# Attention and low-rank FFN block on one core: keys' transposes moved behind the product of probabilities and values, and two PSUM banks exchanged

## The reference

```
x  = x + attn(layernorm(x))          # one pre-norm block
x  = x + ffn(layernorm(x))

attn: xn = layernorm(x) * ln_g + ln_b
      q, k, v = split(xn @ W_qkv + b_qkv);  gate = sigmoid(x @ W_gate + b_gate)
      gate = gate / (mean(gate) + EPS)
      q = relu(q * gate)**2 + EPS;  k = relu(k * gate)**2 + EPS   # 16 heads of 32
      causal linear attention: state += k v^T, sums += k
      out = (q . state) / (q . sums + EPS);  out @ W_proj + b_proj
ffn:  P = x @ U1;  H = gelu(P @ V1 + b1);  Q = H @ U2;  Q @ V2 + b2   # rank 128, 2048 wide
```

## Time and profile before

| what | before |
|---|---|
| median of 3 runs | 1751.72 us (1750.33 to 1752.75) |
| the profiled execution | 1750.89 us |
| its span | 1749.2 us |
| granted TensorE clock, mean | 0.997 |
| matmul / weight load | busy 98% / 82% of the span |
| VectorE / ScalarE / GpSimd | busy 77% / 38% / 52% |
| chain that ended last | TensorE 83%, VectorE 6%, GpSimd 6%, issue 3%, ScalarE 2% |
| an even step with all its parts | 25.37 us (29 of them, all within 25.19 to 25.39) |
| an odd step with all its parts | 27.77 us (29 of them, 27.74 to 27.79) |

### The profile page before, as it was taken

How to read it: one execution, slowest core, us unless ns; L and a number is a source line. 1 busy time by engine, 2 the same in 40 slices (tenths; PEclk the granted TensorE clock), 3 DMA queues, 4 the chain that set the end, 5 groups by cost and what they waited for, 6 DMA issues and landing times.

```text
span 1749.2 us, 39518 instructions
## 1 busy us (share of the span) xinstructions
PE 1714.2 (98%) x16477; PEld 1429.6 (82%) x16477; DVE 1345.2 (77%) x2159; ACT 665.5 (38%) x1242; POOL 911.4 (52%) x1026
## 2 busy tenths in 40 slices
PE   6899999999999999999999999999999999999997
PEld 4788888888888888888888888888888888888886
DVE  7887777877877777777778777778777777777775
ACT  4243343343333343433433433333333434334332
POOL 3355555555555555555555555555555555555540
PEclk9999999999999999999999999999999999999999
DMA  7111111011111111110111111111111111101100
GB/s 218 58 35 52 34 53 45 28 53 53 33 53 39 35 52 36 49 52 23 51 52 33 53 40 33 52 52 34 52 35 39 53 36 50 52 22 52 40 19 25
DMA packets 61937, 82.09 MB, mean 47 GB/s; under 512 B 14952, under 2 KB 25600, under 8 KB 61760
## 3 DMA queue, kind: packets, MB, share of 16 engines
q1 hardware_dynamic: 60896, 77.99, 14.0%
q10 hardware_dynamic: 864, 1.57, 0.3%
HBM read 62.60 MB, written 16.94 MB: 45 GB/s over the span
## 4 chain that ended last, share of the span: by engine, by line
PE 83%; DVE 6%; POOL 6%; issue 3%; ACT 2%; DMA 0%; SPq 0%; DVEq 0%; POOLq 0%
PE ps_a L822 8%; PE ps_a L823 8%; PE ps_a L824 8%; PE scores L822 8%; PE scores L823 8%; PE scores L824 8%; POOL h_lo L432 6%; PE scores L829 5%; PE ps_h L822 5%; PE scores L956 4%; PE scores L991 4%; PE ps_h L823 3%; PE ps_h L824 3%; PE ps_q L822 3%; PE ps_q L824 2%
## 5 line engine op out<-in xcount | busy, mean ns | idle before, releaser
L432 POOL TENSOR_TENSOR h_lo<-h_full,h_hi 128x512 fp32r<-128x512 f32 x244 | 352.0, 1457 | 234.7 <-DVE h_hi L654 234.7
L515 ACT ACTIVATE h_full<-ps_h,cols 128x256 f32<-128x256 f32 x512 | 207.3, 477 | 20.3 <-PE ps_h L824 19.6
L822 PE MATMUL scores<-wx_hi,zt_hi 128*128 128x512 f32 x512 | 207.2, 405 | 6.9 <-DVE key_sums L762 4.3
L822 PE MATMUL ps_a<-wx_hi,zt_hi 128*128 128x512 f32 x512 | 208.4, 407 | 0.0
L823 PE MATMUL scores<-wx_lo,zt_hi 128*128 128x512 f32 x512 | 203.6, 398 | 0.0
L824 PE MATMUL scores<-wx_hi,zt_lo 128*128 128x512 f32 x512 | 203.4, 397 | 0.0
L823 PE MATMUL ps_a<-wx_lo,zt_hi 128*128 128x512 f32 x512 | 202.1, 395 | 0.0
L824 PE MATMUL ps_a<-wx_hi,zt_lo 128*128 128x512 f32 x512 | 201.9, 394 | 0.0
L452 POOL TENSOR_TENSOR key_lo<-keys,key_hi 128x512 fp32r<-128x512 f32 x64 | 83.2, 1300 | 191.1 <-ACT key_hi L550 191.1
L654 DVE CAST h_hi<-h_full 128x512 fp32r<-128x512 f32 x256 | 165.0, 672 | 10.3 <-ACT h_full L515 10.3
L526 ACT ACTIVATE query_t<-scores 128x512 f32<-128x512 f32 x64 | 38.3, 598 | 346.6 <-PE scores L829 346.6
(11 more groups left out here) (158 smaller groups left out, 4283.0 us busy)
## 6 DMA issues: line engine op xcount, KB each, us to landing
xs<-L_attn_x SPq DMA_DIRECT2D x64, 256.0 KB, 4.1
out<-x1s SPq DMA_DIRECT2D x64, 256.0 KB, 2.1
xt<-x_turned SPq DMA_DIRECT2D x63, 256.0 KB, 4.2
key_sums<-carry_rows SPq DMA_DIRECT2D x60, 256.0 KB, 3.8
rows<-turned_rows SPq DMA_DIRECT2D x63, 64.0 KB, 4.8
x1s<-L_attn_W_gate SPq DMA_DIRECT2D x4, 256.0 KB, 3.9
x1s<-L_ffn_U SPq DMA_DIRECT2D x4, 256.0 KB, 7.0
carry_rows<-key_sums SPq DMA_DIRECT2D x64, 2.0 KB
```

Source lines behind the costliest of these rows:

```text
L432: E.tensor_tensor(h_lo[:, i % SLOTS, :], h_full[:, i % SLOTS, :], h_hi[:, i % SLOTS, :].bitcast(F32), ALU.subtract).then_inc(s["h_lo_ready ...
L515: last = E.activation(h_full[:, i % SLOTS, a * GROUP:(a + 1) * GROUP], ps_h[i % 2][:, a * GROUP:(a + 1) * GROUP], ACT.Gelu_apprx_tanh, bia ...
L822: E.matmul(ps, wh, mh, start=start and i == 0, stop=False)
```

## The change

Four things are moved. The keys' transposes and ScalarE's copy `key_t` are done one step ahead, for chunk `n` instead of `c`: TensorE transposes directly behind the product of probabilities and values, into `ps_a`, waiting for `value_ready` and `key_ready`; ScalarE copies behind `ot_hi`. Banks `ps_a` and `ps_b` are exchanged for GATE, KEY, QUERY, the causal sums and the output projection (VALUE stays in `ps_a`). The scores therefore wait for the keys' evacuation instead of the queries', and the VALUE projection for the queries'; the sums wait for `key_t_ready` instead of `ot_ready`. In even steps a second h pair comes ahead of the scores instead of behind them. On VectorE the first cast to `h_hi` (in even steps the first two) comes directly behind `probs`, ahead of the values.

```diff
@@ scalar, step @@
-                if c.exists:
-                    act.wait_ge(s["tk_done"], c.done())
-                    E.activation(key_t[:, :, :].rearrange(flat), ps_t[:, :], ACT.Copy)\
-                        .then_inc(s["key_t_ready"], 1)
...
                     E.activation(ot_hi[:, :, :], out_cols, ACT.Copy)\
                         .then_inc(s["ot_hi_ready"], 1)
+                if n.exists:
+                    act.wait_ge(s["tk_done"], n.done())
+                    E.activation(key_t[:, :, :].rearrange(flat), ps_a[:, :], ACT.Copy)\
+                        .then_inc(s["key_t_ready"], 1)
                 z_head(Chunk(p, b + 1))
@@ vector, step @@
                         .then_inc(s["probs_ready"], 1)
+                if ffn.exists:
+                    h_head(ffn, pairs[0], finishing)
+                    if b % 2 == 0:
+                        h_head(ffn, pairs[1], finishing)
...
-                if ffn.exists:
-                    h_head(ffn, pairs[0], finishing)
                 if c.exists:
                     dve.wait_ge(s["ot_hi_ready"], c.done())
...
                 z_tail(Chunk(p, b + 1))
                 if ffn.exists:
-                    h_head(ffn, pairs[1], finishing)
+                    if b % 2:
+                        h_head(ffn, pairs[1], finishing)
@@ tensor, step @@
-                    project(GATE, ps_b, s["gate_done"])
+                    project(GATE, ps_a, s["gate_done"])
...
-                    project(KEY, ps_a, s["key_done"])
+                    project(KEY, ps_b, s["key_done"])
...
-                    project(QUERY, ps_b, s["query_done"])
-                if c.exists:
-
-                    if d.exists:
-                        pe.wait_ge(s["x1t_ready"], d.done())
-                    else:
-                        pe.wait_ge(s["query_t_ready"], c.done())
-                    pe.wait_ge(s["key_ready"], c.done())
-                    transpose4(keys[:, c.half, :], s["tk_done"])
+                    project(QUERY, ps_a, s["query_done"])
...
                 if ffn.exists and b % 2 == 0:
                     h_pair(ffn, pairs[0])
+                    h_pair(ffn, pairs[1])
                 if c.exists:
 
                     if n.exists:
-                        pe.wait_ge(s["query_steps"], n.done(3, 1))
-                    else:
-                        pe.wait_ge(s["den_steps"], c.done(6, 1))
+                        pe.wait_ge(s["key_steps"], n.done(3, 1))
+                    elif d.exists:
+                        pe.wait_ge(s["x1_steps"], d.done(3, 1))
                     pe.wait_ge(s["key_t_ready"], c.done())
+                    pe.wait_ge(s["query_t_ready"], c.done())
+                    if d.exists:
+                        pe.wait_ge(s["x1t_ready"], d.done())
...
-                if ffn.exists:
-                    h_pair(ffn, pairs[0 if b % 2 else 1])
+                if ffn.exists and b % 2:
+                    h_pair(ffn, pairs[0])
...
-                    pe.wait_ge(s["key_steps"], n.done(3, 1))
+                    pe.wait_ge(s["query_steps"], n.done(3, 1))
                     project(VALUE, ps_a, s["value_done"])
...
                     mm.then_inc(s["ot_done"], 1)
+                if n.exists:
+                    pe.wait_ge(s["value_ready"], n.done())
+                    pe.wait_ge(s["key_ready"], n.done())
+                    transpose4(keys[:, n.half, :], s["tk_done"], ps_a)
...
-                    if c.exists:
-                        pe.wait_ge(s["ot_ready"], c.done())
-                    else:
-                        pe.wait_ge(s["query_steps"], n.done(3, 1))
+                    pe.wait_ge(s["key_t_ready"], n.done())
                     pe.wait_ge(s["key_lo_ready"], n.done())
-                    E.matmul(ps_b[:, :], causal_r[:, :], key_hi[:, :], start=True, stop=False)
+                    E.matmul(ps_a[:, :], causal_r[:, :], key_hi[:, :], start=True, stop=False)
...
-                    product(ps_a[:, :], [(ot_hi[:, k, :], ot_lo[:, k, :]) for k in range(KT)],
+                    product(ps_b[:, :], [(ot_hi[:, k, :], ot_lo[:, k, :]) for k in range(KT)],
```

More of the change, by code:

```diff
@@ L679, in step @@
                     dve.wait_ge(s["x_small"], n.done(5, 2))
-                    E.scalar_tensor_tensor(out=gate[:, :], in0=ps_b[:, :], scalar=small[:, n.slot, 1:2],
+                    E.scalar_tensor_tensor(out=gate[:, :], in0=ps_a[:, :], scalar=small[:, n.slot, 1:2],
                                            in1=bias[:, GATE, :], op0=ALU.mult, op1=ALU.add)\
@@ L692, in step @@
                         add_rows(0)
-                    squared_relu(n, s["key_done"], s["key_steps"], ps_a, KEY, keys[:, n.half, :],
+                    squared_relu(n, s["key_done"], s["key_steps"], ps_b, KEY, keys[:, n.half, :],
                                  x1t_tail)
@@ L711, in step @@
                         add_rows(1)
-                    squared_relu(n, s["query_done"], s["query_steps"], ps_b, QUERY, queries[:, :])
+                    squared_relu(n, s["query_done"], s["query_steps"], ps_a, QUERY, queries[:, :])
                 if b % 2 and ffn.exists:
@@ L789, in step @@
                         dve.wait_ge(stored[c.slot], before.dmas())
-                    E.tensor_tensor(x1s[:, c.slot, :], ps_a[:, :], xs[:, c.slot, :], ALU.add)\
+                    E.tensor_tensor(x1s[:, c.slot, :], ps_b[:, :], xs[:, c.slot, :], ALU.add)\
                         .then_inc(s["x1_steps"], 1)
@@ L825, in product, with transpose4 @@
                 return mm
-            def transpose4(src, done):
+            def transpose4(src, done, ps=ps_t):
                 for k in range(KT):
-                    mm = E.transpose(ps_t[:, k * P:(k + 1) * P], src[:, k * P:(k + 1) * P], ident[:, :])
+                    mm = E.transpose(ps[:, k * P:(k + 1) * P], src[:, k * P:(k + 1) * P], ident[:, :])
                 mm.then_inc(done, 1)
@@ L996, in step @@
                     mm.then_inc(s["ot_done"], 1)
+                if n.exists:
+                    pe.wait_ge(s["value_ready"], n.done())
+                    pe.wait_ge(s["key_ready"], n.done())
+                    transpose4(keys[:, n.half, :], s["tk_done"], ps_a)
                 if ffn.exists:
-                    if b % 2:
-                        h_pair(ffn, pairs[1])
-                    h_pair(ffn, pairs[2])
-                    if b % 2 == 0:
-                        h_pair(ffn, pairs[3])
+                    h_pair(ffn, pairs[1 if b % 2 else 2])
+                    h_pair(ffn, pairs[2 if b % 2 else 3])
                 if n.exists:
-                    if c.exists:
-                        pe.wait_ge(s["ot_ready"], c.done())
-                    else:
-                        pe.wait_ge(s["query_steps"], n.done(3, 1))
+                    pe.wait_ge(s["key_t_ready"], n.done())
                     pe.wait_ge(s["key_lo_ready"], n.done())
-                    E.matmul(ps_b[:, :], causal_r[:, :], key_hi[:, :], start=True, stop=False)
-                    E.matmul(ps_b[:, :], causal_r[:, :], key_lo[:, :], start=False, stop=True)\
+                    E.matmul(ps_a[:, :], causal_r[:, :], key_hi[:, :], start=True, stop=False)
+                    E.matmul(ps_a[:, :], causal_r[:, :], key_lo[:, :], start=False, stop=True)\
                         .then_inc(s["sums_done"], 1)
```

8 lines of the change are left out of this document (2 added, 6 removed).

## The result

| what | before | after |
|---|---|---|
| median of the runs | 1751.24 us (6, 1750.33 to 1752.75) | 1744.18 us (6, 1743.48 to 1744.5) |
| ratio after / before | | 0.9958, 95% interval 0.9945 to 0.997 |
| the profiled execution, its span | 1750.89, 1749.2 | 1743.48, 1741.7 |
| an even step | 25.37 | 24.76 |
| an odd step | 27.77 | 28.19 |

The kernel is 7.1 us (0.4%) faster by the medians and 7.5 us by the two spans. It is less than the even steps alone gained: 30 x 0.61 = 18.3 us, of which 31 odd steps of +0.42 took 13 back; the ends gave the other 2. All lengths of steps and parts here are means over the 29 even and 29 odd steps with all their parts, as distances between two starts; within one kernel they scatter by a few hundredths, but for single even steps of the kernel before and of e11, up to 0.2 us shorter than the others.

A forecast was written before the change was run, and what follows sets the result against it. TensorE, busy 1714.2 of 1749.2 us, was taken as the bound; 30 even steps by -0.60, 31 odd by +0.51 and -3 for the ends sum to -5.2 us, from 1751.7 to 1747 us, range 1738 to 1757.

The forecast's parts named there:

- even: transposes and their wait taken out ahead of the scores: Even step, ahead of the scores: the four transposes gone, -0.44 us, and the wait for `key_t` gone, -0.13 us.
- even: transposes behind the product: Even step, behind the product of probabilities and values: the four transposes put in cost +0.44 us, bounds +0.34 and +0.64.
- even: sums without `ot_lo`: Even step, the sums' first matmul: it no longer waits for `ot_lo`, -0.11 us.
- even: u2 products: Even step, u2 products: early casts let GpSimd's last `h_lo` end some 1.5 us earlier, removing a wait, -0.36 us.
- odd: gain left ahead of the first h pair: Odd step, scores to first h pair: `pt_lo` on VectorE leaves only 0.10 of the transposes' 0.44 us as gain.
- odd: gelu behind `ot_hi`: Odd step, last h pair: its gelu comes later by 0.49 us for copy `key_t` and about 0.12 for the transposes.
- ends: First and last steps: about -2 us in step 64, -1 in steps 1 and 2; together -3.
- Rival (d): Around the moved transposes: the change of products costs twice, +0.2 us in both kinds of step; 1759 us, chance 0.06.
- the +0.12 for `key_t` waiting on the transposes: Odd step, ScalarE: `key_t` cannot start before the transposes are done, making the last h pair's gelu about 0.12 us later.
- (a): Even step, VectorE: early casts meet GpSimd, values come late and TensorE's transposes wait; 1756 us with one held, chance 0.12.
- (b): Odd step: the last h pair's new wait does not come, the gelu being done in time; 1731 us, chance 0.10.
- (c): Even step: last `h_lo` stays late, held by GpSimd or delayed gelus, so 0.36 us stays; 1758 us, chance 0.07.

The follow-up runs named there:

- e11: The kernel before with only banks `ps_a` and `ps_b` exchanged and the waits that follow; 1750.35 us, ratio 0.9991 to before.
- e1: The kernel after with the keys' transposes and copy `key_t` back at their old place behind the QUERY projection; 1736.43 us, ratio 0.991 to before.
- e3: The kernel after with `pt_lo` put ahead of the queries' third operation on VectorE in odd steps; 1734.33 us, ratio 0.9897 to before.
- e2: The kernel after with the second pair's gelu put ahead of `zt_hi` on ScalarE in odd steps; 1752.97 us, ratio 1.0006 to before.
- e6: The kernel before with only the early casts to `h_hi` moved directly behind the masking; 1741.45 us, ratio 0.994 to before.
- e9: The kernel after; in odd steps second pair's gelu ahead of `zt_hi`, its cast ahead of `zt_lo`, `pt_lo` ahead of the queries' third operation; 1734.45 us.
- e12: The kernel after; odd steps: second pair's gelu ahead of `zt_hi`, second and third pairs' casts ahead of `zt_lo`, `pt_lo` before queries' third operation; 1728.07 us.

## Why the prediction was right, point by point

The forecast was a change of -5.2 us against the profiled execution; the spans differ by -7.5, and the median, 1744.18, lies 2.8 below the 1747 said and inside the range. The even step came as worked out, the odd one by the waits that were worked out and a little cheaper.

| term | forecast | measured |
|---|---|---|
| even: transposes and their wait taken out ahead of the scores | -0.57 | -0.57 |
| even: transposes behind the product | +0.44 | +0.41 |
| even: sums without `ot_lo` | -0.11 | -0.11 |
| even: u2 products | -0.36 | -0.34 |
| **even step** | **-0.60** | **-0.61** |
| odd: gain left ahead of the first h pair | -0.10 | -0.14 |
| odd: gelu behind `ot_hi` | +0.61 | +0.55 |
| **odd step** | **+0.51** | **+0.42** |
| ends | -3 | -2.2 |

**Taking out the transposes.** Measured as one sum, since the h pair moved as well: transposes -0.35, the two h pairs (1.03 + 0.82 before, 1.51 after) -0.33, and VALUE, which now stands right behind small products, +0.11. The 0.13 us of wait had two owners, which the prediction left open: e11, in which the scores wait for the keys' evacuation, has 0.05 of it less. The rest fits the copy `key_t` and was not tested apart.

In e1 the transposes stand at the old place again; there they cost the even step 0.35 us and the h pairs behind them 0.08 (1.59 instead of 1.51 for the two), near the 0.44 of the forecast.

**Transposes behind small products.** The prediction took +0.44 between +0.34 and +0.64: the transposes with the dearer first matmul behind them, while the 0.10 us that the h pair paid behind small products passes to them. Measured are 0.41 us from the first transpose to the h pair, 0.06 more than between full products, and the pair's first matmul still takes 0.20 (841.94 to 842.14) instead of 0.12. So the change from small to full products was paid once, as said, at 0.06 instead of 0.10 us. Rival (d) did not come.

**The odd step.** That its first h pair meets `pt_lo` and its last one a later gelu is shown twice: by the releasers, and by e3 and e2, which each took one wait away at its place (that e2 lost more elsewhere does not change this). The term that was mis-sized is the +0.12 for `key_t` waiting on the transposes: `ot_hi` to `key_t` took 0.55 us, only 0.06 more than the 0.49 of plain copies. The rest of the 0.09 is the 0.04 more that was gained ahead of it. Over 31 steps it is 2.7 us, most of the distance between forecast and result.

**Ends.** Step 64 was forecast at -2 and gave about -0.9, counted from its start (1704.09 before, 1697.48 after) to the next transposes of `zs`. TensorE's timeline in it, before:

```profile
1710.57 2.09 PE L956 MATMUL scores<-query_t,key_t 32*128 32x128 f32 x32
...
1715.08 0.51 PE L985 MATMUL scores<-query_t,state 32*32 32x128 f32 x32 [0.80 <-DVE probs L720]
```

and after:

```profile
1702.59 1.17 PE L955 MATMUL scores<-query_t,key_t 32*128 32x128 f32 x32
...
1706.17 0.59 PE L984 MATMUL scores<-query_t,state 32*32 32x128 f32 x32 [2.02 <-DVE probs L720]
1706.69 1.94 PE L990 MATMUL scores<-probs,values 128*32 128x128 f32 x32
```

The table by windows (us, then busy time and count of TensorE, its weight load, VectorE, ScalarE and GpSimd, the granted clock, the DMA share and GB/s), one window before and two after:

```profile
1710.00:1713.30 3.30, 3.30 (x39) 2.85 (x38) 0.57 (x1) 1.14 (x3) 0.00 (x0) 0.50 0.00 0
```

```profile
1704.40:1706.40 2.00, 0.23 (x29) 0.23 (x32) 2.00 (x2) 0.00 (x0) 0.00 (x0) 1.00 0.00 0
1706.50:1709.80 3.30, 3.30 (x64) 2.63 (x39) 2.38 (x5) 0.60 (x1) 0.00 (x0) 0.50 0.02 5
```

The second h pair did fill the wait: the scores start 5.1 us behind the step's start instead of 6.5, and the products with the state 8.7 instead of 11.0, a gain of 2.3 us up to there. Of this some 1.4 us went again behind it. The h pair no longer stands between the scores and the products with the state, which wait for the masking, so TensorE stood idle for 2.02 us there instead of 0.80. After that wait the granted clock was 0.50, the level of 1.2 GHz: the product of probabilities and values lasted 1.94 us where it takes 1.0 elsewhere, and the two h pairs 2.11 instead of 1.53. Before, the clock was at that level earlier in the step, at the scores, which lasted 2.09 instead of 1.17 us. The prediction counted a wait as gone without asking what its filling had covered, and what is late next. The other 1.3 us of the ends, which were not taken apart, lie in the first and last steps.

**The rivals.** (a) did not come: the casts took 0.76 us together, and the values started at 812.62, in time; only in the very first step did the transposes wait for the values. But it was near. GpSimd's last operation ahead of them after, and VectorE's two casts and GpSimd's operation beside them in an even step of e6:

```profile
810.54 1.30 POOL L413 TENSOR_TENSOR xt<-xt,rows 128x512 f32<-128x512 f32 x1
```

```profile
864.03 2.17 DVE L654 CAST h_hi<-h_full 128x512 fp32r<-128x512 f32 x2
864.46 1.47 POOL L413 TENSOR_TENSOR xt<-xt,rows 128x512 f32<-128x512 f32 x1
```

In the kernel after, the centering ends at 811.84 and the first cast starts at 811.85. With the transposes at the old place the casts met GpSimd and took 1.76 us (e1) and 2.17 us (e6) together, more than the 1.7 that the prediction set as the limit; there no transpose waits for the values. So the reason given against (a), that `key_hi` and GpSimd come earlier with the copy moved, fits (`key_lo` starts 11.6 us behind the step's start after, 13.2 in e6), but that GpSimd would be done only 0.01 us ahead of the casts was not worked out, and that much is luck. A cast held for some tenths would still have been covered: the values end at 813.37 and the transposes start at 814.36. The mechanism shows in the odd step of e9 as well, in which `zt_lo` was held for 1.83 - 0.69 = 1.14 us. The Trainium skill, "SBUF — State Buffer", section "SBUF: two separate sides", has an exclusive lock of the port shared by VectorE and GpSimd; the 1.83 us beside an `h_lo` of 1.30 agree with it: `zt_lo` ends 0.55 us behind the `h_lo`, where it takes 0.69 alone. (b) did not come by itself, and e2 shows that it would not have been a gain: with the gelu's wait gone, GpSimd's came. (c) did not come, with 2 us to spare. Not foreseen was how little room there was behind the waits, which only the runs showed.

**What stays open.** The old place (e1) was not run together with e12's orders on VectorE and ScalarE, and the second h pair ahead of the scores was not run apart. Whether 24.8 and 27.6 us are the floor of the steps isn't known either.

## What to carry to other kernels

Before a product is moved to where an engine's own order looks free, ask for every consumer behind it which of its waits already ends with zero slack; here the place with 0.1 us to gain was left for one with two such waits, and the casts, a side edit, carried the gain. An earlier release is worth only what the next engine in the chain can use: move the whole chain (gelu, cast, low part) or none of it. Test the parts of a combined change alone and in pairs, since one part can earn next to nothing without the other (the banks without the casts) and another can cost what the rest earns (the transposes).

## What the runs showed of the hardware

A two-input VectorE operation of 0.69 us (`zt_lo`) lasted 1.83 us in e9, where it started 0.02 us after a GpSimd `h_lo` of 1.30 us, and 0.68 us in e12, where it ran ahead. The other way round GpSimd pays: its `h_lo` took 1.68 us instead of 1.30 where `zt_lo` was ahead. Which engine was first hung, in these two runs, on one cast in VectorE's order. GpSimd's `h_lo` starts about 0.1 us behind the end of its cast (812.35, the first cast ending near 811.85 + 0.41), while VectorE's next operation, if it waits for nothing, starts before that end, so two casts in a row took 0.76 us in the kernel after. Four transposes of 128x128 float32 cost 0.35 us between full products and 0.41 us behind 32-wide ones.
